# Splitting the dispatched rows at the sender and loading them transposed, in a gated attention and mixture-of-experts block

## What is computed

```python
x = x + tanh(g_xattn) * (softmax(q(layernorm(x)) @ k(ctx).T / sqrt(128)) @ v(ctx) @ Wo.T + bo)
xn = layernorm(x)
probs = softmax(xn @ gate_w.T)
topk_probs, topk_idx = top_k(probs, 2)
h = gelu(xn @ w1[:, e].T + b1[e])          # e = each of the two chosen experts, width 512
y = h @ w2[:, e].T + b2[e]
x = x + tanh(g_ffn) * sum(y * topk_probs)
```

## Time and profile before

| | us |
|---|---|
| median of 3 runs | 103.05 (102.95 to 103.39) |
| the profiled execution | 102.97 |
| its span, first to last instruction | 101.2 |
| busy: PE, DVE, POOL, ACT | 79.3, 64.5, 51.2, 49.6 |

### The profile page before, as it was taken

How to read it: one execution, slowest core, us unless ns; L and a number is a source line. 1 busy time by engine, 2 the same in 40 slices (tenths; PEclk the granted TensorE clock), 3 DMA queues, 4 the chain that set the end, 5 groups by cost and what they waited for, 6 DMA issues and landing times.

```text
span 101.2 us, 2701 instructions
## 1 busy us (share of the span) xinstructions
PE 79.3 (78%) x773; PEld 65.4 (65%) x773; DVE 64.5 (64%) x271; ACT 49.6 (49%) x149; POOL 51.2 (51%) x78
## 2 busy tenths in 40 slices
PE   5849877579997330397599999999999999999800
PEld 1248455366965320122369999999999999999700
DVE  2078899885449469549865656558987665145570
ACT  4133579796841920700076757657475665750000
POOL 6866603367788877740000746466463645600570
PEclk9995899965555555569999999999999999999996
DMA  0999998901110012921454464010101011019424
GB/s 15 326 370 440 427 408 312 341 17 59 53 53 26 26 59 81 218 69 32 112 116 89 110 160 108 15 39 26 34 26 58 12 32 42 26 39 266 141 80 130
DMA packets 11662, 12.65 MB, mean 125 GB/s; under 512 B 1379, under 2 KB 10615, under 8 KB 11392
## 3 DMA queue, kind: packets, MB, share of 16 engines
q1 hardware_dynamic: 9808, 9.74, 30.6%
q0 software_dynamic: 1120, 2.12, 7.0%
q10 hardware_dynamic: 720, 0.62, 2.2%
HBM read 8.18 MB, written 4.48 MB: 125 GB/s over the span
## 4 chain that ended last, share of the span: by engine, by line
PE 43%; DMA 15%; DVE 15%; POOL 12%; issue 6%; ACT 3%; SPq 1%; POOLq 1%; DVEq 0%
PE bank L714 18%; POOL dispatched L357 6%; PE bank L700 5%; PE bank L702 5%; DMA res<-results 5%; PE bank L701 4%; DMA wp<-in_wpack 4%; PE bank L689 3%; POOL rstd L393 3%; DMA dispatched<-rows,slot 2%; DVE xn L780 2%; PE bank L617 2%; DMA results<-y_sb,in_rows 2%; DVE x L838 2%; DMA in_rows<-dispatched 2%
## 5 line engine op out<-in xcount | busy, mean ns | idle before, releaser
L537 ACT ACTIVATE hid<-bank,wp 128x128 f32<-128x128 f32 x92 | 26.3, 368 | 21.1 <-PE bank L702 20.2
L427 POOL DMA_INDIRECT results<-y_sb,in_rows x19 | 18.9, 993 | 25.0 <-DVE y_sb L981 25.0
L714 PE MATMUL bank<-w_sb,hid 128*128 x184 | 25.6, 282 | 0.0
L714 PEld LDWEIGHTS bank<-w_sb,hid 128*128 128x128 f32 x184 | 22.4, 192 | 0.0
L357 POOL DMA_INDIRECT dispatched<-rows,slot x16 | 15.8, 988 | 4.7 <-issue 3.9
L700 PE MATMUL bank<-xs_t,w_hi 128*128 128x128 f16 x92 | 17.1, 220 | 0.1
L701 PE MATMUL bank<-xs_t,w_hi 128*128 128x128 f16 x92 | 17.1, 219 | 0.0
L702 PE MATMUL bank<-xs_t,w_lo 128*128 128x128 f16 x92 | 17.1, 219 | 0.0
L546 PE MATMUL bank<-ones 128*128 128x512 bf16 x26 | 8.9, 509 | 5.9 <-DVE tile_rows L955 4.7
L975 DVE COPY xs_t<-bank 128x256 f16<-128x256 f16 x23 | 6.7, 291 | 7.0 <-PE bank L689 6.5
L546 PEld LDWEIGHTS bank<-ones 128*128 128x128 bf16 x26 | 2.9, 123 | 11.0 <-issue 8.3
(11 more groups left out here) (150 smaller groups left out, 144.7 us busy)
## 6 DMA issues: line engine op xcount, KB each, us to landing
w_sb<-in_w SPq DMA_DIRECT2D x2, 2048.0 KB, 11.7
in_rows<-dispatched SPq DMA_DIRECT2D x23, 65.0 KB, 1.9
results<-zeros SPq DMA_DIRECT2D x1, 1024.0 KB, 10.6
res<-results SPq DMA_DIRECT2D x4, 256.0 KB, 4.7
ctx_sb<-in_ctx_t SPq DMA_DIRECT2D x1, 512.0 KB, 5.7
out<-out_sb SPq DMA_DIRECT2D x4, 128.0 KB, 1.9
wp<-in_wpack ACTq DMA_DIRECT2D x1, 342.0 KB, 4.0
dispatched<-pad_rows SPq DMA_DIRECT2D x5, 65.0 KB, 3.7
```

The lines of the kernel that those rows point to most:

```text
L427: pool.indirect_dma_start(results_dram, bass.IndirectOffsetOnAxis(ap=in_rows[:].bitcast(U32)[:, t, TARGET:TARGET + 1], axis=0), y_sb[:, t, ...
L537: mm = act.activation(hid[:, t % HIDS, b, :], hid_ps[t % HID_PS][:, b * P:(b + 1) * P], ACT.Gelu_apprx_tanh, bias=b1[:, bass.ds(experts[t] ...
L714: mm = pe.matmul(to, hid[:, t % HIDS, b, :], w2_sb[:, bass.ds(e, 1), b * P:(b + 1) * P], start=False, stop=b == BLOCKS - 1)
```

## The change

The sender splits each row into halves. `fill_rows` now makes two activations for a tile: the f32 value once into a new array `xn2`, and its f16 rounding twice into the first half of the row. VectorE subtracts the two and writes the low half (`low_halves`, steps LOW_A and LOW_B of TIMES, one for each tile of a group). A row in HBM is as long as before: 128 f16 high, 128 f16 low, target, gate.

SP loads the 256 f16 values of each of the 128 rows by a transposing DMA, straight into `xs_t`, which now holds all 23 tiles. Target and gate of a tile come by a second DMA of 8 bytes a row into `marks`, issued six tiles behind (MARKS_BEHIND). `split_rows`, `turn_rows`, `copy_rows`, `ident16` and `parts` are gone. `hidden` waits for the transposed load, `gated` for the marks. The one-hots move from the 10th iteration to the 14th; they need the marks of the last four tiles. TIMES has new values for nearly all steps.

```diff
@@ constants and TIMES
-LAST, ONE_HOTS = 4, 10
+MARKS_BEHIND = 6
+LAST, ONE_HOTS = 4, 14
...
-    ROOT: [16.4, 20.4, 29.1, 32.6],
+    ROOT: [16.5, 21.1, 30.2, 36.2],
...
-    ROWS: [18.6, 25.1, 32.2, 34.1],
+    ROWS: [21.2, 23.5, 32.0, 37.8],
+    LOW_A: [22.0, 24.8, 32.9, 38.9],
+    LOW_B: [23.8, 26.1, 33.4, 39.3],
...
@@ SP
-            for t in range(N_TILES):
-                if t >= AHEAD and t % LOADS == 0:
+            for t in range(N_TILES + MARKS_BEHIND):
+                if AHEAD <= t < N_TILES and t % LOADS == 0:
                     first = list(first) + list(table_values(sp, tile_rows, PAD_ROW, t))
-                sp.dma_start(in_rows[:, t, :], rows_dram[bass.ds(first[t], SLOT_TILE), :]).then_inc(loaded[t], 16)
+                if t < N_TILES:
+                    sp.dma_start_transpose(xs_t[:, t, :, :], halves_dram[bass.ds(first[t], SLOT_TILE), 0:2 * P]).then_inc(loaded[t], 16)
+                u = t - MARKS_BEHIND
+                if u >= 0:
+                    sp.dma_start(marks[:, u, :], rows_dram[bass.ds(first[u], SLOT_TILE), P:ROW]).then_inc(marked[u], 16)
@@ ScalarE, fill_rows
-                    act.activation(row_f[:, t, :, 0:P], x1[:, t, None, :].to_broadcast((P, TOP_K, P)), ACT.Identity,
-                                   bias=nbias[:, t:t + 1], scale=rstd2[:, t:t + 1]).then_inc(rows_ok, 1)
+                    act.activation(xn2[:, t, :], x1[:, t, :], ACT.Identity, bias=nbias[:, t:t + 1],
+                                   scale=rstd2[:, t:t + 1]).then_inc(halves_ok, 1)
+                    act.activation(row_h[:, t, :, 0:P], x1[:, t, None, :].to_broadcast((P, TOP_K, P)), ACT.Identity,
+                                   bias=nbias[:, t:t + 1], scale=rstd2[:, t:t + 1]).then_inc(halves_ok, 1)
@@ TensorE
             def hidden(t, e):
-                pe.wait_ge(xs_ok, t + 1)
-                hi, lo = xs_t[:, t % XS, 0, :], xs_t[:, t % XS, 1, :]
+                pe.wait_ge(loaded[t], 16)
+                hi, lo = xs_t[:, t, 0, :], xs_t[:, t, 1, :]
...
-            for t in range(LAG):
-                turn_rows(t)
             pe.wait_ge(w1_ok, PARTS)
             for t in range(N_TILES + LAG + 1):
                 if t < N_TILES:
                     hidden(t, experts[t])
-                if t + LAG < N_TILES:
-                    turn_rows(t + LAG)
@@ VectorE
+            def low_halves(t):
+
+                v.wait_ge(halves_ok, 2 * (t + 1))
+                v.tensor_tensor(row_h[:, t, :, P:2 * P], xn2[:, t, None, :].to_broadcast((P, TOP_K, P)), row_h[:, t, :, 0:P],
+                                ALU.subtract).then_inc(rows_ok, 1)
...
             def gated(t):
                 v.wait_ge(y_in_ps, t + 1)
-                gate = in_f[:, t, GATE:GATE + 1]
+                v.wait_ge(marked[t], 16)
+                gate = marks_f[:, t, 1:2]
...
                 for t in range(SCATTERED, N_TILES):
-                    v.wait_ge(loaded[t], 16)
+                    v.wait_ge(marked[t], 16)
```

More of the change, by code:

```diff
@@ new lines @@
+    NORM_T: [7.5, 9.4, 11.5, 15.2],
+    COPY_NORM_T: [8.1, 9.9, 12.7, 16.7],
+    QUERIES: [8.7, 10.9, 13.3, 18.0],
+    COPY_QUERIES: [9.5, 11.7, 14.5, 22.7],
+    SCORES: [10.4, 12.2, 16.2, 23.2],
+    MAXIMUM: [11.3, 12.8, 18.3, 24.2],
+    EXPONENT: [12.1, 13.8, 19.2, 25.0],
+    PROBS_T: [12.9, 14.7, 19.9, 25.9],
+    COPY_PROBS_T: [13.4, 15.9, 20.8, 27.2],
+    VALUES: [9.8, 8.1, 22.0, 27.6],
+    COPY_VALUES: [10.5, 8.8, 23.1, 28.7],
+    X_BIAS: [13.4, 13.7, 14.0, 14.3],
+    ATTEND: [14.0, 16.7, 24.0, 29.6],
@@ new lines @@
+    RESIDUAL: [14.8, 17.5, 25.3, 30.9],
+    X1_T: [15.7, 18.6, 26.7, 31.9],
+    COPY_X1_T: [16.3, 19.8, 27.6, 33.5],
+    STATS: [15.6, 20.2, 27.5, 33.8],
+    ROOT: [16.5, 21.1, 30.2, 36.2],
+    NBIAS: [18.9, 22.5, 31.7, 37.3],
+    ROWS: [21.2, 23.5, 32.0, 37.8],
+    LOW_A: [22.0, 24.8, 32.9, 38.9],
+    LOW_B: [23.8, 26.1, 33.4, 39.3],
+    ROUTE: [17.4, 20.7, 28.6, 34.0],
+    CHOOSE: [19.1, 22.6, 29.7, 35.1],
+    EXP_LOGITS: [20.3, 25.7, 31.3, 37.3],
+    RANKS: [20.4, 25.2, 31.0, 36.4],
@@ L98 @@
+    FILL: [20.9, 26.6, 32.0, 37.9],
+    SEND_A: [22.6, 27.7, 33.7, 39.7],
+    SEND_B: [25.2, 31.2, 37.2, 42.3],
+    W1_HIGH: [14.9, 17.0, 18.1, 26.1],
+    W1_LOW: [16.4],
+    NUMBERS: [11.9],
 }
@@ L222, in gated_block @@
         whose = sb("whose", [P, LAST, TOKENS], F16)
-        row_f, in_f = rows[:].bitcast(F32), in_rows[:].bitcast(F32)
+        row_f, row_h, marks_f = rows[:].bitcast(F32), rows[:].bitcast(F16), marks[:].bitcast(F32)
+        halves_dram = rows_dram.bitcast(F16)
         res = sb("res", [P, TILES, TOP_K, P], F32)
@@ L272, in gated_block @@
         w1hi_ok, w1_ok, b2hi_ok, b2_ok = sem("w1hi_ok"), sem("w1_ok"), sem("b2hi_ok"), sem("b2_ok")
-        loaded = [sem(f"loaded{t}") for t in range(N_TILES)]
-        parts_ok, xs_in_ps, xs_ok, hid_in_ps, hid_ok = sem("parts_ok"), sem("xs_in_ps"), sem("xs_ok"), sem("hid_in_ps"), sem("hid_ok")
+        loaded, marked = [sem(f"loaded{t}") for t in range(N_TILES)], [sem(f"marked{t}") for t in range(N_TILES)]
+        hid_in_ps, hid_ok = sem("hid_in_ps"), sem("hid_ok")
         y_in_ps, y_ok = sem("y_in_ps"), sem("y_ok")
@@ L922, in _ @@
                     weights_lo(w1_lo, w1_sb, w1_hi, w1hi_ok, w1_ok, g)
+                elif step == LOW_A:
+                    low_halves(STARTS[g])
+                elif step == LOW_B:
+                    low_halves(STARTS[g] + 1)
                 elif step == FILL:
@@ L992, in last_tokens @@
                 for t in range(SCATTERED, N_TILES):
[L993 to L994 removed]
+                    v.wait_ge(marked[t], 16)
+                n = then(v.tensor_scalar(last_i[:], marks[:, SCATTERED:N_TILES, 0], 1, None, ALU.logical_shift_right))
                 v.wait_ge(dve, n)
@@ L1007, in base_sum @@
                 return then(v.tensor_tensor(out_sb[:, q, :], out_sb[:, q, :], res[:, q, 1, :], ALU.add))
-            for t in range(N_TILES + LAG):
-                if t == 0:
-                    for u in range(LAG):
-                        split_rows(u)
-                    for u in range(LAG):
-                        copy_rows(u)
-                    bias_low()
-                    split_rows(LAG)
-                if t + LAG < N_TILES:
-                    copy_rows(t + LAG)
-                if t + LAG + 1 < N_TILES:
-                    split_rows(t + LAG + 1)
-                if t >= LAG:
-                    gated(t - LAG)
+            bias_low()
+            for t in range(N_TILES):
+                gated(t)
                 if t == ONE_HOTS:
```

82 lines of the change are left out of this document (15 added, 67 removed).

## The result

The changed kernel takes 120.1 us (median of 4 runs, 119.6 to 121.4), the kernel before, on the same chip, 103.0 us (102.2 to 103.4): a ratio of 1.165, with a 95% interval of 1.155 to 1.175. The forecast was 99.3 us, its range ended at 104.5: wrong in direction and in size. The profiled execution took 120.36 us with a span of 118.6 us. I compare it with the span of 101.2 us before.

The account below looks back on a forecast made before the run. It took POOL's sends, then the handover, a full TensorE and a tail as the bound. Gating 18 4.35 us earlier plus 0.6 of queue wait made -3.75 us on 102.97, so 99.3 us by the median; range 98.4 to 104.5.

Parts of the forecast that it names:

- What bounds the kernel, the handover's chain and the tail: Whole kernel: attention, then POOL's sends, the handover to the experts, TensorE full from 53.36 to 85.56 us, a 14.4 us tail.
- Part 4, the queue: SP's queue: 46 loads instead of 23, transposing issues 0.1 us dearer; TensorE waits at output 17, +0.6 us.
- The break-even at 0.26 us: SP's queue: a transposing issue near 0.26 us above a plain one would cancel the gain.
- no wait, 0.7 us to spare: Loop start: small load 0 issued at 51.4, landing at 53.3, in time for output 2 at 54.5.
- The rival: SP's queue: transposing loads are dear; each 0.1 us per issue makes the last small load 2.3 us later; chance 0.27.
- Part 1, the sender: Routing before the experts: an added activation and subtraction per tile delay the first send from 22.02 to 22.37, +0.35 us.
- 0.9 us of cover is left: Sender's end: the pad transfers land by 45.5 us, just ahead of the last send at 46.35.
- The third rival: Sender: pads or VectorE's table come last instead of POOL, 0.9 us more per 0.9 us beyond the cover; chance 0.08.
- Part 2, the handover: From sends to experts: transposing loads bring the first output to 51.1 instead of 53.36 us, headed -2.4 us.
- The sum of -4.35: Expert loop's end: gating of tile 18 at 82.4 instead of 86.77 us if nothing holds TensorE up.
- Part 3, the loop: Expert loop: two transposes a tile leave TensorE, 18 intervals of 1.67 instead of 1.789 us, -2.1 us.
- The clock: First expert tiles: a late first load lets idle TensorE return to the lower clock, 100.2 to 103.2 us; chance 0.10.

Follow-up runs that it names:

- kernel 1: The changed kernel with plain loads in place of the 23 transposing ones, so rows reach the experts untransposed; 100.5 us.
- kernel 11: The changed kernel with each send's two waits swapped, first for the row's second half, then for its slot; 118.0 us in one run.
- kernel 7: The kernel before with its eight pad transfers issued only when the tile table is ready; 105.6 us.
- kernel 10: The changed kernel with all small loads on ScalarE's queue, the last four early, and group 3's root ahead of group 2's low halves and sends; 101.4 us.
- Kernel 4: The changed kernel's sender and order, but rows loaded whole by plain DMAs and transposed on TensorE as in the kernel before; 104.4 us.
- kernel 6: The changed kernel with all small loads issued on ScalarE's queue, four ahead, SP issuing only the transposing loads; 106.2 us.
- kernel 12: kernel 10 with the two waits of each send swapped as in kernel 11; 101.2 us.

## Why the prediction was wrong, step by step

**What bounds the kernel, the handover's chain and the tail**: right. The tail behind gating 18 was 13.5 us instead of 14.4.

**Part 4, the queue: the step that failed.** "For the transposing issue I take 0.1 us above the plain one", from a 2 MB load that holds the queue for 0.45 us. Measured 0.84 above (1.17 against 0.33), 0.78 over the whole queue in kernel 1. That is outside even my upper bound of 0.75. 23 x 0.68 us more than taken are 15.6 us. The rest of the queue, 28.4 us in my sum (30.7 less 23 x 0.1), was 30.6 in kernel 1: 2.2 us more. Together that is the 18.0 us measured. The form of the argument held: the count of issues, the last small load as the one that ends it, VectorE behind gating 14, output 17 behind gating 15. The break-even at 0.26 us no run tests. At the start of the loop I had "no wait, 0.7 us to spare": small load 0 was issued at 59.76 and not at 51.4, and output 2, due at 54.5, began at 62.12. The rival's own rule, 2.3 us later for each 0.1 us, gives from 103.9 at +0.3 some 115 us at +0.78; the start of SP (2.3), the rest of the queue (2.2) and the clock (1.6), less the shorter tail (0.9), are the rest of the way to 120. What was wrong was the row chosen: a load's size tells how long a plain issue lasts, and a transposing instruction is another kind. No row of it existed, and the nearest by kind, POOL's send, "the only other descriptor-rich issue", stood at the top of my bounds, where it would have put the case on the other side. A chance of 0.27 on the rival was too low, as nothing in the profile separated 0.1 from 0.75.

The Trainium skill (Advanced Engine Details and Errata, X-Bar Transpose (TRN2)) says that a transposing DMA is as fast as a regular one. The landing bears that out roughly (2.4 against 1.9 us); the queue does not (1.17 against 0.33 us). The same page's table DGE: Hardware vs Software, which gives the hardware's transposes the worse efficiency, pointed the right way, though no run here has a transposing load of the other kind to set beside it.

**Part 1, the sender: +0.35 taken, more measured.** The durations were near: the 128x128 activation 0.48 us (0.42 taken), the subtraction 0.42 as taken, and the low half there at 22.18 (I had 22.07). Three terms were missing. (a) The send started 0.95 us after its release and not 0.3, because it stands behind two waits of which the second one blocks: 0.6 us, shown by kernel 11. (b) In groups 2 and 3 one send each came 1.49 us after the one before instead of 1.27: 0.4 us. The profile names the second tile's low half as what released it, which I had held covered; but the 0.22 us lie in the length of the send before it (1.18 and 1.19 us instead of 0.96), and whether the low half is the cause is not shown. (c) "0.9 us of cover is left" for the pads was no cover. They do not have to land after the last send to cost: written beside it, they make it land later. The last send's landing took 3.73 us instead of 2.50, 1.2 us more. That pads closer to the last send do this is shown by kernel 7; kernel 10 puts them back to the distance of before, and the landing took 2.74 us. The counts started at 40.8 and not at 39.5. The third rival had the right place, but was priced as an overrun of the cover. Kernel 4 puts the sender's whole price at 2.7 us at gating 18 and 1.6 us of time.

**Part 2, the handover.** The transposing landing: 2.2 taken, 2.4 measured. The filling matmuls, however, started at 44.80 (43.6 taken) and ran at the lower clock until about 49.7 us. First expert matmul at 51.65, first output at 55.25 (taken 49.0 and 51.1), the latter because loads 1.3 us apart cannot feed hidden layers of 0.67. "If the loads come 0.6 us apart" was a condition, and it failed with part 4. (The heading's -2.4 us does not match its own numbers: 53.36 - 51.1 is 2.3. The sum of -4.35 was made with 2.3.)

**Part 3, the loop: right,** once the queue is out of the way: 1.67 us a tile in kernels 1, 6, 10 and 12.

**The clock.** I had named its fall for the first tiles. It fell at about 63 us, after TensorE had stood for 2.8 us behind small load 0, and rose again at about 67; that costs nothing at the end, since the small loads set the pace there. And it fell while TensorE stood for 5.3 us behind the last small load: 1.6 us.

## What to carry to other kernels

Before a transfer changes its kind, ask what one issue of it costs the queue, not only how long it takes to land, and if the trace has no row of that kind, treat the whole width of the bounds as likely. Count all that stands in that queue per tile and hold it against the time of a tile: 1.30 us alone fits into 1.67 (1.56 to 1.64 on average, with all that delays it), 1.92 with a small load does not, and the remedy was another queue. And a transfer that runs beside the last one before a handover has a price even when it lands first, because the last one then lands later.

## What the runs showed of the hardware

- A transposing load's issue on SP's queue lasts 1.17 us for 128 rows of 512 bytes, 1.11 for half of that. Issues behind each other come every 1.30 us. Of more or fewer rows no run tells.
- The transfer itself is not the limit: between 50 and 60 us of the changed kernel, where SP issues one transposing load after another, the DMA engines were busy for 0.22 of the time.
- Small loads of 8 bytes a row hold the queue like a load of 64 KB: 0.33 us among plain loads, 0.42 among transposing ones, 0.34 on ScalarE's queue.
- Now and then an issue lasts longer for no reason that the trace shows: 2.33 us for the fifth transposing load of the changed kernel, 2.63 in kernel 6, 2.00 once for a plain one. The fifth load of kernel 6 and the fourth of kernel 12 stand in the chain with 4.2 and 4.4 us to their landing. What causes it stays open.
- In kernel 7, sends land 2.3 to 2.5 us after their start while no pads are written, 3.9 to 4.5 us beside the 65 KB pad transfers of two queues.
- The first indirect send, behind two waits, starts 0.3 us after its release if the second wait is met already (the kernel before, kernels 11 and 12), 0.95 us if it is the second that blocks (the changed kernel). Other sends do not test it.
